# Two-layer cross-attention with experts: the first keys' preparation at other places, the key normalisation in halves, and routed rows normalised one tile a step

## The reference

```python
x = x + _L0_xattn_ref(_layernorm(x), ctx, ctx, ...)        # correlation attention by FFT, best 4 shifts
x = x + _L0_ffn_ref(_layernorm(x), ...)                    # two layers with quantised rows and ternary weights, GELU
x = x + _L1_xattn_ref(ctx, _layernorm(x), ...)             # 16 heads, keys = 64 context rows and 64 rows of x
x = x + _L1_ffn_ref(_layernorm(x), ...)                    # 8 experts, the best 2 of a row
```

```python
x = layer_norm(image_embeds, ln1_g, ln1_b)
l = layer_norm(latents, ln2_g, ln2_b)
q = l @ Wq
kv = concatenate([x, l], axis=1) @ Wkv
w = softmax(q k^T)
```

## Time and profile before

| | |
|---|---|
| median of 3 runs | 1555.33 us (1554.91 to 1556.73) |
| profiled execution | 1558.58 us, span of its instructions 1556.8 us |
| busy, share of the span | PE 88%, DVE 84%, ACT 81%, PEld 74%, POOL 70% |
| instructions | PE 16544, DVE 3902, ACT 3873, POOL 1515 |
| mean granted clock of TensorE | 0.952 of full speed |
| DMA | 110.29 MB, mean 71 GB/s |

### The profile page before, as it was taken

One profiled execution on the slowest core, in us unless ns is written; L12 is line 12 of the kernel. 1 busy time (PEld: TensorE's weight loads), 2 busy tenths in 40 slices (PEclk: granted clock), 3 DMA queues, 4 the chain that ended last, 5 costly groups with the idle time before them and its releaser, 6 DMA issues. The chain is left out here.

```text
span 1556.8 us, 51025 instructions
## 1 busy us (share of the span) xinstructions
PE 1370.0 (88%) x16544; PEld 1158.9 (74%) x16544; DVE 1308.8 (84%) x3902; ACT 1262.3 (81%) x3873; POOL 1085.9 (70%) x1515
## 2 busy tenths in 40 slices
PE   4798899976999999999999999999999929999960
PEld 3677777755788888888888888888888717888850
DVE  3689999987899999999999999999989826777757
ACT  2388888875999999999999999999999917777745
POOL 2478876755466688788788887878887754777760
PEclk9899999986999999999999999999999968999985
DMA  5345644221010111111011111111110014445419
GB/s 157 118 177 206 247 153 164 87 65 28 5 25 20 28 31 36 26 29 33 23 32 29 36 26 30 31 30 27 27 34 21 23 34 77 93 93 86 86 36 324
DMA packets 171728, 110.29 MB, mean 71 GB/s; under 512 B 104953, under 2 KB 152604, under 8 KB 171569
## 3 DMA queue, kind: packets, MB, share of 16 engines
q1 hardware_dynamic: 151968, 86.90, 19.6%
q0 software_dynamic: 8640, 16.93, 3.7%
q10 hardware_dynamic: 10960, 4.46, 1.0%
HBM read 30.09 MB, written 57.16 MB: 56 GB/s over the span
## 5 line engine op out<-in xcount | busy, mean ns | idle before, releaser
L1415 ACT ACTIVATE c_p<-bank,c_nmax 128x128 f32<-128x128 f32 x1024 | 364.4, 386 | 1.7 <-DVE c_nmax L1268 1.7
L1206 POOL TENSOR_TENSOR c_p<-c_p,c_rden 128x512 f32<-128x512 f32 x256 | 266.6, 1041 | 106.5 <-DVE c_rden L1286 100.0
L1415 ACT ACTIVATION_READ_ACCUMULATOR c_p<-bank,c_nmax 128x1 f32 x1024 | 233.3, 228 | 0.0
L1577 POOL DMA_INDIRECT moe_outputs<-e_y,e_to x142 | 159.7, 1125 | 75.1 <-issue 45.2
L1268 DVE TENSOR_REDUCE c_nmax<-bank 128x4 f32<-128x512 f32 x256 | 173.6, 678 | 20.2 <-PE bank L114 20.2
L112 PE MATMUL bank<-turned,qk_fused 128*128 128x128 f16 x1024 | 184.5, 219 | 2.7 <-PEq L249 1.7
L114 PE MATMUL bank<-turned,qk_fused 128*128 128x128 f16 x1024 | 184.6, 219 | 0.0
L113 PE MATMUL bank<-turned,qk_fused 128*128 128x128 f16 x1024 | 184.6, 219 | 0.0
L1465 PE MATMUL bank<-const,c_p 128*128 128x128 f32 x1024 | 156.7, 275 | 20.1 <-DVE c_pT0rest L1297 19.8
L1639 ACT ACTIVATE e_h<-bank,moe_b 128x256 f32<-128x256 f32 x284 | 117.9, 465 | 52.2 <-PE bank L114 46.4
L1251 POOL DMA_INDIRECT moe_slots<-r_rows,r_pos x128 | 131.6, 1028 | 34.3 <-issue 34.3
(11 more groups left out here) (341 smaller groups left out, 5789.3 us busy)
## 6 DMA issues: line engine op xcount, KB each, us to landing
moe_slots<-slot_fill SPq DMA_DIRECT2D x66, 520.0 KB, 5.7
f_z<-moe_outputs SPq DMA_DIRECT2D x32, 256.0 KB, 4.9
x<-in_x SPq DMA_DIRECT2D x16, 256.0 KB, 3.2
context_rows<-in_ctx SPq DMA_DIRECT2D x32, 128.0 KB, 3.2
moe_stage<-in_L_ffn_W SPq DMA_DIRECT2D x16, 256.0 KB, 3.2
context_rows<-in_ctx SPq DMA_DIRECT2D x64, 64.0 KB, 2.3
context_rows<-x SPq DMA_DIRECT2D x64, 64.0 KB, 2.0
out_x<-x ACTq DMA_DIRECT2D x16, 256.0 KB, 6.4
```

The costliest lines, as they stand in the source:

```text
L1206: pool.tensor_tensor(pr[r % 4][:], pr[r % 4][:], rep(rden[r % 4][:], 2, P), ALU.mult).then_inc(m["pn"], 1)
L1415: last = act.activation(pr[r % 4][:, h, :], SB[r % 2][:, P * h:P * h + P], ACT.Exp, bias=nmax[r % 4][:, h:h + 1], accum_out=den[r % 4][:, ...
L1577: pool.indirect_dma_start(s.z, bass.IndirectOffsetOnAxis(ap=to[t % YBUF][:, h:h + 1], axis=0), ys[t % YBUF][:, h, :], None, bounds_check=2 ...
```

## The change

1. VectorE takes the statistics of the first four key tiles in step 16 of the first layer, behind `hidden` and ahead of `add_out`, and no longer at the end of step 17; and in step 18 it does `hidden` ahead of `key_norm`.
2. GpSimd does `hidden_scale` ahead of `key_scale` in step 17 and ahead of all `key_parts` in step 18. `key_parts` of tiles 2 and 3, and SP's turns of these, move behind the barrier, to the start of the cross-attention's block.
3. In the cross-attention key statistics and reciprocal root come four steps earlier (19 and 17). The normalisation is cut in two: the first half at 16, the second at 13, both behind VectorE's three rests of their step. Each tile has its own statistics buffer.
4. ScalarE normalises one routed tile a step in four steps (28 to 31) in groups 0 to 12, and TensorE turns them at 32, not 30. The last three groups keep their places.

```diff
@@ -129,6 +129,19 @@
         sp.dma_start(to[rows, :, half, :], s.xg(n // 2)[rows, 2 * (n % 2):2 * (n % 2) + 2, :]).then_inc(s.key_loaded[n % 2], 16)
+
+
+def key_parts(pool, s, v):
+
+    if v == 0:
+        pool.wait_ge(s.w_norm, 16 * 9)
+    pool.wait_ge(s.key["kvn"], v + 1)
+    pool.tensor_tensor(s.kv[v], s.kv[v], s.ln_g[:], ALU.mult)
+    pool.drain()
+    pool.tensor_tensor(s.kvs[v][:, 0, :, :], s.kv[v], s.ln_b[:], ALU.add)
+    pool.tensor_tensor(s.kv[v], s.kv[v], s.ln_b[:], ALU.add)
+    pool.drain()
+    pool.tensor_tensor(s.kvs[v][:, 1, :, :], s.kv[v], s.kvs[v][:, 0, :, :], ALU.subtract).then_inc(s.key["kv"], 1)
 
@@ -392,7 +405,7 @@
                 load_keys(sp, s, dram["ctx_1024"], n)
-            for v in range(AHEAD):
+            for v in range(2):
                 turn_keys(sp, s, v)
@@ -492,17 +505,6 @@
                 pool.tensor_tensor(s.key_rstd[:], s.key_rstd[:], s.mhalf[:].rearrange("p (t n) -> p t n", n=2), ALU.pow).then_inc(s.key["rstd"], AHEAD)
-
-            def key_parts(v):
-                if v == 0:
-                    pool.wait_ge(s.w_norm, 16 * 9)
-                pool.wait_ge(s.key["kvn"], v + 1)
-                pool.tensor_tensor(s.kv[v], s.kv[v], s.ln_g[:], ALU.mult)
-                pool.drain()
-                pool.tensor_tensor(s.kvs[v][:, 0, :, :], s.kv[v], s.ln_b[:], ALU.add)
-                pool.tensor_tensor(s.kv[v], s.kv[v], s.ln_b[:], ALU.add)
-                pool.drain()
-                pool.tensor_tensor(s.kvs[v][:, 1, :, :], s.kv[v], s.kvs[v][:, 0, :, :], ALU.subtract).then_inc(s.key["kv"], 1)
 
@@ -517,16 +519,13 @@
                     split_weights(i, k, 2 * i + k - 1)
+                if a := at(i, k, -3):
+                    hidden_scale(a[0], a[1])
                 if known(i) and 2 * i + k == GROUPS + 1:
...
                     for v in range(2):
-                        key_parts(v)
-                if a := at(i, k, -3):
-                    hidden_scale(a[0], a[1])
-                if known(i) and 2 * i + k == GROUPS + 2:
-                    for v in range(2, AHEAD):
-                        key_parts(v)
+                        key_parts(pool, s, v)
             pool.memset(ip[:], 0.0)
@@ -705,11 +704,17 @@
                     invert(a[0], a[1])
+                if a := at(i, k, -3):
+                    hidden(a[0], a[1], at(i, k, 0))
+                if known(i) and 2 * i + k == GROUPS:
+                    for v in range(AHEAD):
+                        key_stats(v)
+                    dve.drain()
+                    for v in range(AHEAD):
+                        key_moments(v)
                 if known(i) and 2 * i + k == GROUPS + 2:
...
                         key_norm(v)
-                if a := at(i, k, -3):
-                    hidden(a[0], a[1], at(i, k, 0))
                 if a := at(i, k, 0):
@@ -723,11 +728,6 @@
                 if known(i) and 2 * i + k == GROUPS + 1:
-                    for v in range(AHEAD):
-                        key_stats(v)
-                    dve.drain()
-                    for v in range(AHEAD):
-                        key_moments(v)
                     dve.wait_ge(b1_t, 1)
@@ -1101,7 +1101,6 @@
         norm_mul, norm_add = s.norm_mul, s.norm_add
-        bst = s.key_bn[:, 0, :, :]
         mv = [s.key_mv[:, n, :, :] for n in range(4)]
@@ -1157,14 +1156,16 @@
 
-        AT_STATS, AT_RSTD, AT_KVN, AT_KV, AT_G, AT_S, AT_PN, AT_PT, AT_O, AT_W, AT_X3 = 15, 13, 12, 11, 6, 3, 2, 0, -1, -5, -9
+        AT_STATS, AT_RSTD, AT_KVN, AT_KV, AT_G, AT_S, AT_PN, AT_PT, AT_O, AT_W, AT_X3 = 19, 17, 16, 11, 6, 3, 2, 0, -1, -5, -9
         EVEN = GROUPS - 3
         ROUTE_STATS = 10
-        ROUTE_RSTD, ROUTE_XN, ROUTE_XT, ROUTE_LOGITS = (23, 23, 23), (28, 28, 24), (30, 29, 25), (34, 30, 26)
+        ROUTE_RSTD, ROUTE_XT, ROUTE_LOGITS = (23, 23, 23), (32, 29, 25), (34, 30, 26)
+        ROUTE_XN = [(28 + j, 28, 24) for j in range(GT)]
         ROUTE_TOP, ROUTE_INDEX, ROUTE_MASK = (35, 31, 27), (38, 32, 28), (39, 32, 28)
...
         AT_KV_LOW = AT_KV - 1
+        AT_KVN_SECOND = AT_KVN - 3
         ROUTE_SCATTER = tuple(zip((44, 46, 47, 48, 50, 51, 52, 54), (39, 40, 42, 43, 44, 46, 47, 48), (33, 34, 35, 36, 38, 39, 40, 41)))
@@ -1190,10 +1191,11 @@
         def _(sp):
-            for v in range(AHEAD, TILES):
-                sp.wait_ge(m["s"], 4 * (v - 3))
+            for v in range(2, TILES):
+                if v >= AHEAD:
+                    sp.wait_ge(m["s"], 4 * (v - 3))
                 turn_keys(sp, s, v)
-                if v % 2 == 1 and v + 3 < TILES:
+                if v % 2 == 1 and AHEAD < v and v + 3 < TILES:
                     sp.wait_ge(m["kvn"], v + 1)
@@ -1250,6 +1252,9 @@
                                             rows[q][:, j, :], None).then_inc(scattered[q], 16)
+            pool.drain()
+            for v in range(2, AHEAD):
+                key_parts(pool, s, v)
             walk(pool, FIRST, LAST, 16, LO, HI, step)
@@ -1266,14 +1271,6 @@
                     dve.tensor_reduce(nmax[r % 4][:], SB[r % 2][:].rearrange("p (h c) -> p h c", h=4), AX.X, ALU.max, negate=True).then_inc(m["max"], 1)
-                if t := fresh(i, k, AT_KVN):
-                    v, r, g = t
-                    a, b = mv[r], rst[r]
-                    dve.wait_ge(m["rstd"], v + 1)
-                    wait(dve, m["kv"], v - 3)
-                    for n in range(2):
-                        last = dve.tensor_scalar(kv[r][:, n, :], cs[r // 2][:, r % 2, n, :], a[:, n, 0:1], b[:, n:n + 1], ALU.subtract, ALU.mult)
-                    last.then_inc(m["kvn"], 1)
                 if (g := group(i, k, ROUTE_TOP)) is not None:
@@ -1301,8 +1298,18 @@
                     dve.tensor_tensor(lo, OB[:].rearrange("p (h c) -> p h c", h=8), hi, ALU.subtract).then_inc(m["o_copied"], 1)
+                if t := fresh(i, k, AT_KVN):
+                    v, r, g = t
+                    dve.wait_ge(m["rstd"], v + 1)
+                    wait(dve, m["kv"], v - 3)
+                    dve.tensor_scalar(kv[r][:, 0, :], cs[r // 2][:, r % 2, 0, :], mv[r][:, 0, 0:1], rst[r][:, 0:1], ALU.subtract, ALU.mult)
+                if t := fresh(i, k, AT_KVN_SECOND):
+                    v, r, g = t
+                    dve.tensor_scalar(kv[r][:, 1, :], cs[r // 2][:, r % 2, 1, :], mv[r][:, 1, 0:1], rst[r][:, 1:2],
+                                      ALU.subtract, ALU.mult).then_inc(m["kvn"], 1)
                 if t := fresh(i, k, AT_STATS):
                     v, r, g = t
+                    bst = s.key_bn[:, r, :, :]
                     dve.wait_ge(c_loaded[r // 2], 64 * (g + 1))
@@ -1423,12 +1430,14 @@
                     act.activation(rows[own(g)][:, :, 0:D], r_xn[:], ACT.Copy).then_inc(mr["row_high"], 1)
-                if (g := group(i, k, ROUTE_XN)) is not None:
-                    act.wait_ge(mr["rstd"], g + 1)
-                    wait(act, mr["row_done"], g)
-                    for j in range(GT):
+                for j in range(GT):
+                    if (g := group(i, k, ROUTE_XN[j])) is not None:
+                        if j == 0:
+                            act.wait_ge(mr["rstd"], g + 1)
+                            wait(act, mr["row_done"], g)
                         last = act.activation(r_xn[:, j, :], s.xg(g)[:, j, :], ACT.Identity, bias=r_nb[:, j:j + 1], scale=r_rstd[:, j:j + 1])
-                    last.then_inc(mr["xn"], 1)
+                        if j == GT - 1:
+                            last.then_inc(mr["xn"], 1)
             walk(act, FIRST, LAST, 16, LO, HI, step)
```

## The result

The change takes 1538.34 us in the median of six runs (1533.70 to 1545.70), the kernel before 1555.35 (1554.31 to 1556.73): 0.9898 of it, 95% interval 0.9872 to 0.9925, so 17.0 us less. The forecast was 1531 (range 1511 to 1551), 24 us less. The profiled execution took 1535.22 us, span 1533.4, at a mean clock of 0.961.

What follows compares the result with a forecast made beforehand. TensorE was taken to lead the cross-attention (busy 800 of 820 us), its 43 waits for VectorE's rests costing 32 us. Terms 6.2 + 16 + 2 = 24.2 us off the median 1555.3 gave 1531, range 1511 to 1551.

Steps and rivals of the forecast that it cites:

- Statistics in step 16, parts behind the barrier: Passage to cross-attention: both moves cost nothing; 1.3 us to spare before the first product of probabilities.
- Hidden scale: Passage, group 14: GpSimd's scale starts at 354.0 instead of 360.22, so 6.2 us gained; nothing counted for group 15.
- the paragraph on the clock: Passage: if TensorE stays at 2.4 GHz, 12.00 us of matmuls become 6, the passage gives 12.2, total 1525.
- my sum leaves the clock low: Passage: idle stretch shrinks to about 1.8 us, but the sum of 1531 assumes TensorE's clock still falls.
- the upper case: Passage: clock stays at 2.4 GHz and the passage gives 12.2 us, for a total of 1525.
- the term of 16 us: Cross-attention: normalisation in halves, last in the step, recovers half of TensorE's 32 us of waits.
- rival D: Cross-attention: halves meet GpSimd's work, 0.90 us for 0.34, 66 us more on VectorE; slower, 1574; chance 0.08.
- Added: one half at the end of the step before, 0.34 us.: Cross-attention, VectorE: the step before a key step gains one half of the normalisation, taking 0.34 us.
- The saving as 0.34 for the pair and 0.26 for the root on average: Cross-attention key steps: removing pair (0.60) and average root wait (0.26), adding one half (0.34), brings the rest 0.52 us earlier.
- rival B: Cross-attention: VectorE becomes the bound, waits move one step on, only the passage gains 6.2 us; 1549; chance 0.15.
- Key rows four steps earlier: Cross-attention: statistics and reciprocal root earlier cost nothing; key rows land with 3.9 us to spare.
- ScalarE's rows, 2 us: Cross-attention: rows one a step cut VectorE's 6.1 us of waits for the high part; bounds 0 and 6.1, taken 2.

Runs made afterwards that it cites:

- e12: The change again, unedited, beside the kernel before: 20.5 us less, ratio 0.987.
- e10: The change with both halves of a key tile behind the rests of one step (offset 13): 23.0 us less than the kernel before, ratio 0.9862.
- e11: The change with the first half between maximum and reciprocal, without part 4: 21.9 us less than the kernel before, ratio 0.9874.
- e8: The kernel before with only GpSimd's hidden scale ahead of key scale and key parts: 8.9 us less, ratio 0.9945.
- e1: The kernel before with parts 1 and 2 of the change alone: 9.7 us less, ratio 0.9945.
- e9: The kernel before with only key statistics and reciprocal root four steps earlier, pair of halves in place: 15.0 us less, ratio 0.9911.
- e2: The kernel before with part 3 of the change alone: 4.1 us less, ratio 0.9972.
- e4: The change with the first half between maximum and reciprocal (offset 14): 1523.83 us, 32.2 us less than the kernel before, ratio 0.9795.
- e7: The change with the first half written as an instruction with two SBUF inputs: 14.9 us less than the kernel before, ratio 0.9904.
- e5: The change with both halves between maximum and reciprocal, in two steps (14 and 13): 25.7 us less than the kernel before, ratio 0.9835.
- e6: The change with the pair of halves at its old place (offset 12): 29.6 us less than the kernel before, ratio 0.983.

## Why the prediction was right, and where it was not

**Statistics in step 16, parts behind the barrier: nothing, as said.** GpSimd had 1.50 us to spare before the first product of probabilities (forecast 1.3), against the 13.80 of the earlier trace rows.

**Hidden scale: right to 0.2 us.** e12 shows it best, since its first event (316.66) is 0.15 from that before and its clock fell as before:

```profile
354.24 0.20 POOL L471 TENSOR_TENSOR b_tmp<-b_ssq,eps_times_ff 128x4 f32<-128x4 f32 x1 [0.23 <-ACT b_junk L773]
```

```profile
357.68 0.18 DVE L650 RECIPROCAL b_qs<-b_mx 128x4 f32<-128x4 f32 x1 [1.88 <-POOL b_deq L485]
...
382.03 0.35 DVE L612 SCALAR_TENSOR_TENSOR x<-bank,b_deq,x 128x128 f32<-128x128 f32 x1 [0.50 <-PE bank L1018]
```

```profile
383.69 0.27 PE L112 MATMUL bank<-turned,qk_fused 128*128 128x128 f16 x1 [1.70 <-PEq L262]
```

Forecast were 354, 357.5 and, for the first key product, 383.6. The last add is 6.1 us earlier than the 388.11 of before, for 6.2. The first key products then still ran at half clock, so at the first maximum 5.0 are left. Where the fused weights kept 2.4 GHz it was 9.7 us, for the 12.2 that the paragraph on the clock worked out: there group 14's quantisation came 7.1 us earlier against the first event (353.81 - 313.80 for 363.66 - 316.51).

**The clock: both cases happen, and the waits tell them apart.** TensorE's turn of group 14 (L1008) in e12 and in the change's first profile, and there that of group 15:

```profile
359.92 1.30 PE L1008 MATMUL bank<-ident_f,b_gelu 128*128 128x128 f16 x16 [1.89 <-DVE b_gelu L655]
```

```profile
356.04 1.07 PE L1008 MATMUL bank<-ident_f,b_gelu 128*128 128x128 f16 x16 [0.82 <-DVE b_gelu L655]
...
368.99 1.89 PE L1008 MATMUL bank<-ident_f,b_gelu 128*128 128x128 f16 x16 [4.54 <-DVE b_gelu L655]
```

The forecast had 1.8 us of idle time ahead of group 14's turn. Of the nine profiles with the new passage three have 1.89 or 1.90 (e10, e11, e12), and in all three the clock fell within 1.1 us of the turn's start and the fused weights ran at 1.2 GHz. In the other six it was 0.82 to 0.97 us (1.41 in e8), and the clock stayed at 2.4 GHz for the fused weights. There it had been low for 3.4 us just ahead, so that TensorE's earlier products ended later and the wait was the shorter one. So "my sum leaves the clock low" was right for the idle time that it had, but the wrong side for the median: -9.7 in e1 is nearer the upper case. In that case TensorE then stands 4.54 us for group 15's quantisation, and the clock falls there for 10.2 us. The prediction counted nothing for group 15; with the clock up that is late next, and one reason for 9.7 in place of 12.2.

The clock was low for 41.0 us in six profiles: the four with the old passage, e10 and e12. In just these six it had also fallen for 3.4 us at 34.5 to 36.7 us of the span, and in no other. What decides is thus there near the start already; why is open. Between e12's profile and the change's first one the passage differs by 4.7 us and the start by 2.9, 7.6 of the 12 us over which the change's runs spread. Its two longest runs had mean clocks of 0.952 and 0.953, the other four 0.959 to 0.961, which fits; but those two have no profile.

**The halves: the term of 16 us failed.** Parts 3 and 4 gave 10.6 and 7.8 us in two profiles, for 18; part 3 alone 4.1 by the median and 2.5 by the stage. Two steps of the working were wrong.
- *"Added: one half at the end of the step before, 0.34 us."* It took 0.82 us on average from 414 us on. That is the mechanism of rival D, on one of the two halves: 23 us more on VectorE (71.5 - 48.3) where D had 66 for all, so VectorE's 41 us of waits could pay it and the time did not turn. The rows of the passage to it were there (1.15 us at 915.21), but I took the median of a place where GpSimd stands waiting, for a place where it works.
- *The saving as 0.34 for the pair and 0.26 for the root on average.* e9 shows that the wait was the costly part: 15.4 us of it gave 15.0 us. It fell in 20 of 60 key steps, up to 1.9 us at a time, and 17 of those 20 made TensorE wait, where of the 39 steps with the pair alone 25 did, for shorter times (8.9 us in all). Averaging it over 60 steps hid that.

Late next, as rival B had it, was VectorE at the head of the next step, but not at the same wait: the addition to x and the maximum. How much of the 11 us between e9 and e2 is the longer half and how much its place isn't separated: e10 removes the length but puts two halves in one step.

**Key rows four steps earlier: nothing, as said.** No wait for them is among the change's.

**ScalarE's rows, 2 us:** the median alone -0.2 (interval 0.9979 to 1.0004), the stage -2.5; with the first half ahead of the reciprocal 9. A wait's price depended on which other wait was gone.

The total was right in sign and in size, 17.0 us for 24, but partly by luck: in the profile the passage gave 3.5 us more than the sum, by a clock that the sum had low, and the halves and rows gave 7 to 10 less. The forecast's own mechanism for its largest term, halves of 0.34 us behind the rests, held for the second halves only.

## What to carry to other kernels

Before moving work on VectorE, look at what GpSimd does at the new place, not only at what VectorE does there: an instruction took 0.34 us where GpSimd stood waiting for VectorE, and 0.85 or 1.5 where GpSimd had its product running or ready. The best place for the first half here was between the maximum and the reciprocal, where GpSimd waits for just that reciprocal; both halves there were worse. Take a rare long wait away first, by an earlier producer, and only then shorten what is regular; and try each part with and without the others, since here ScalarE's rows gave 2.5 us of the stage alone and 9 once the first half stood at its best place.

## What the runs showed of the hardware

- A product of GpSimd that is ready holds VectorE's half off even before it starts. Behind a scatter with a ready product next, 58 halves (the change, e2, e4, e7, e12) that began 0.23 to 1.01 us into the scatter waited until the product had ended, up to 2.00 us in all; four that began up to 0.20 us into it took 0.34. Where the product still had to wait for its reciprocal, 15 halves (e5, e6, e9, e10) that began 0.36 to 1.01 us into a scatter took 0.33 to 0.36 us. So GpSimd's product got in first although the half had come earlier, and the scatter by itself held nothing.
- The same program, on the same inputs, had TensorE's clock low for 24 or for 41 us in the passage, and the time differed by 4.7 us there. Behind 8.03 idle us, and behind 1.89 or 1.90, the clock was low for the products that followed, behind 0.82 to 1.41 at the same place it was not.
- On some chips the part behind the 253rd maximum took 48 to 63 us longer with the stages ahead of it unchanged. ScalarE waited 41.3 us for what the profile calls "remote" in e5 from 1285 to 1480 us, and none in e4. The cause is open.
